# Projection, attention and feed-forward net in one block: the first maxima ahead of k's last spread, the first gates behind the last sums, late weights awaited where they are read

## The reference: what is computed

```python
q, k, v = x @ Wq.T + bq, x @ Wk.T + bk, x @ Wv.T + bv      # 16 heads of 16
q, k = rope(q), rope(k)
a = softmax(q @ k.T / sqrt(256)) @ v                        # 4096 x 4096 scores a head
x = layernorm(x + a @ Wo.T)
h = silu((x @ w1.T) * w1_s) * ((x @ w2.T) * w2_s)           # 256 -> 1024
h = gelu((h @ h1.T) * h1_s)                                 # 1024 -> 1024
h = gelu((h @ h2.T) * h2_s)                                 # 1024 -> 1024
x = layernorm(x + (h @ w3.T) * w3_s)                        # 1024 -> 256
```

## Time and profile before

| | us |
|---|---|
| median of 3 runs (3430.74 to 3432.02) | 3431.28 |
| the profiled execution | 3430.39 |
| its span | 3428.8 |
| PE busy | 3345.8 |
| DVE busy | 2985.9 |
| ACT busy | 2490.1 |

### The profile page before, as it was taken

How to read it: one execution, slowest core, us unless ns; L and a number is a source line. 1 busy time by engine, 2 the same in 40 slices (tenths; PEclk the granted TensorE clock), 3 DMA queues, 4 the chain that set the end, 5 groups by cost and what they waited for, 6 DMA issues and landing times. The chain is left out here.

```text
span 3428.8 us, 66866 instructions
## 1 busy us (share of the span) xinstructions
PE 3345.8 (98%) x28054; PEld 1529.5 (45%) x28054; DVE 2985.9 (87%) x3116; ACT 2490.1 (73%) x4521; POOL 128.0 (4%) x288
## 2 busy tenths in 40 slices
PE   9689999999999999999999999999999999999998
PEld 5233333333333333333333333333333288888887
DVE  8899999999999999999999999999999145555554
ACT  5248888888888888888888888888888822222222
POOL 0000000000000000000000000000000000000000
PEclk9679999999999999999999999999999999999999
DMA  4200000000000010001000000000002020000000
GB/s 157 76 4 13 13 12 13 25 13 18 25 12 14 11 62 12 13 13 61 13 13 30 13 13 13 13 12 13 12 8 94 13 91 26 26 26 26 26 13 13
DMA packets 47618, 92.04 MB, mean 27 GB/s; under 512 B 9922, under 2 KB 21828, under 8 KB 47140
## 3 DMA queue, kind: packets, MB, share of 16 engines
q1 hardware_dynamic: 40628, 72.07, 6.7%
q0 software_dynamic: 6688, 15.68, 1.6%
HBM read 69.62 MB, written 28.84 MB: 29 GB/s over the span
## 5 line engine op out<-in xcount | busy, mean ns | idle before, releaser
L886 DVE TENSOR_REDUCE group_max<-wide 128x2 f32<-128x1024 f32 x2048 | 2473.2, 1223 | 16.0 <-PE wide L656 9.4
L857 ACT ACTIVATE probs<-scores 128x512 f32<-128x512 f32 x4046 | 2199.6, 597 | 293.1 <-PE scores L780 41.3
L678 PE MATMUL sums<-probs,v_all 128*17 128x256 f32 (+1 forms) x16120 | 1278.4, 389 | 7.2 <-ACT mixed L837 6.3
L780 PE MATMUL scores<-q_sb,k_all 51*128 51x512 f32 x3968 | 988.6, 495 | 6.7 <-ACT probs L857 5.7
L656 PE MATMUL wide<-k_all,q_sb 48*128 48x512 f32 x4096 | 850.2, 411 | 33.5 <-DVE group_max L886 26.7
L780 PEld LDWEIGHTS scores<-q_sb,k_all 51*128 51x128 f32 x3968 | 370.5, 183 | 842.3 <-ACT probs L857 828.9
L678 PEld LDWEIGHTS sums<-probs,v_all 128*17 128x17 f32 x16120 | 267.1, 95 | 747.3 <-issue 367.5
L656 PEld LDWEIGHTS wide<-k_all,q_sb 48*128 48x128 f32 x4096 | 397.5, 190 | 72.4 <-DVE group_max L886 63.9
L1221 ACT ACTIVATE whole_hid<-acc,scale 128x512 f32<-128x512 f32 x128 | 84.6, 688 | 286.3 <-PE acc L1111 286.1
L1111 PE MATMUL acc<-hid_a,first_h1T 128*128 128x512 f32 x1024 | 233.5, 389 | 2.9 <-issue 2.9
L1111 PE MATMUL acc<-hid_b,h2T 128*128 128x512 f32 x1024 | 234.9, 390 | 0.0
(11 more groups left out here) (121 smaller groups left out, 1075.9 us busy)
## 6 DMA issues: line engine op xcount, KB each, us to landing
q_sb<-q_parts SPq DMA_DIRECT2D x192, 64.0 KB, 2.5
heads<-mixed SPq DMA_DIRECT2D x128, 34.0 KB
xt<-in_xT SPq DMA_DIRECT2D x8, 512.0 KB, 4.4
q_parts<-k_all SPq DMA_DIRECT2D x8, 512.0 KB, 3.3
q_parts<-parts SPq DMA_DIRECT2D x8, 512.0 KB, 3.3
w_words<-in_h1T POOLq DMA_DIRECT2D x32, 128.0 KB, 2.3
w_words<-in_h2T POOLq DMA_DIRECT2D x32, 128.0 KB, 2.3
heads_sb<-heads SPq DMA_DIRECT2D x16, 256.0 KB
```

The lines of the kernel that those rows point to most:

```text
L678: last = pe.matmul(sums[32 * j:32 * j + HD + 1, cols], v_all[:, kt, g, j], probs[(kt * HG + j) % RING][:, cols], start=(kt == 0 and cols.s ...
L780: pe.matmul(scores[(s + e) % BANKS][:], k_all[rows, g * GP + j, n // HG * P:(n // HG + 1) * P], q_sb[g][rows, j], start=True, stop=True).t ...
L857: act.activation(probs[n % RING][:], bank, ACT.Exp, scale=INV_SCALE)\
L886: dve.reduce_max(group_max[:, n], wide[n % 2][:], AX_X).then_inc(wide_free, 1)
```

## The change

One block is opened in `build` and handed to the three functions, so the two barriers between them are gone, and what they ordered is now ordered by semaphores, which live to the end. In `project`, q of group 0 is placed after item 14 is stored, groups 1 to 3 after item 15 is stored; the last spread is handed to `attend` as `before["spread_last"]`, and PE issues it after the first two groups of maxima. SBUF and PSUM tiles are placed in another order, so that what attention writes first doesn't lie on what projection reads last: `table` moves to the end, `probs` behind `bits`, and three of the four PSUM tiles of the spread move to the banks of `scores`. At the net's start PE waits for w1T, w2T and h1T, ACT and DVE for the small tables (before, SP waited for them ahead of the barrier); h2T and w3T are awaited where a layer reads them.

```diff
@@ project
-        block = ctx.enter_context(nc.Block())
...
                     for b in range(2):
                         sp.wait_ge(q_stored[b], 16)
-                    for g in range(NG - 1):
-                        place_q(sp, q_dram, q_sb[g], 0, g, q_in[g])
-            for b in range(2):
-                sp.wait_ge(q_stored[b], 16 * NCH * FT // 2)
+                    place_q(sp, q_dram, q_sb[0], 0, 0, q_in[0])
+
+            sp.wait_ge(v_ready, 2 * NCH)
+            for g in range(1, NG):
+                place_q(sp, q_dram, q_sb[g], 0, g, q_in[g])
...
-            for n in range(TOTAL + 2):
-                if n < TOTAL:
-                    item_of(n)
-                    values(n // FT, n % FT)
+            for n in range(TOTAL):
+                item_of(n)
+                values(n // FT, n % FT)
                 if n >= 2:
-                    spread_k(n - 2)
+                    spread_k(pe, n - 2)
+            spread_k(pe, TOTAL - 2)
@@ attend
-        probs = [sb(f"probs{r}", [P, CH]) for r in range(RING)]
...
         bits = sb("bits", [P, PIECE], I32)
+        probs = [sb(f"probs{r}", [P, CH]) for r in range(RING)]
...
-            load_q(0, NG - 1)
+            for b in range(2):
+                sp.wait_ge(before["q_stored"][b], 16 * (before["total"] // 2))
             place_shift(0, 0)
...
-            sp.wait_ge(w0_in, 16 * len(EARLY_W))
-            sp.wait_ge(small0_in, 16 * SMALL)
...
             pe.wait_ge(ident_set, 2)
+
+            pe.wait_ge(before["spread_free"], before["first_keys"])
+            pe.wait_ge(before["biased"], 2 * before["total"])
+            pe.wait_ge(before["v_free"], 2 * NCH)
             for n in range(MAXG):
                 max_group(0, 0, n)
+                if n == 1:
+                    before["spread_last"](pe)
+            pe.wait_ge(before["spread_free"], before["keys"])
...
+            dve.wait_ge(before["low_done"], before["total"])
             dve.memset(bits[:], 0).then_inc(scanned, 1)
             maxima(0)
 
+            dve.wait_ge(before["spread_free"], before["keys"])
             dve.memset(sums[:], 0.0).then_inc(sums_free, 1)
@@ feed_forward
                 def hidden_layer(c, layer):
+                    if layer == 1:
+
+                        pe.wait_ge(w_in["h2T"], 16)
...
+                    pe.wait_ge(w_in["w3T"], 16)
                     pe.wait_ge(hid_ready, c * HIDS + HIDS - 1)
...
+                pe.wait_ge(fc.w_in, 16 * len(EARLY_W))
                 gate_layer(0)
-                for name in w_in:
-                    pe.wait_ge(w_in[name], 16)
...
+            act.wait_ge(fc.small_in, 16 * SMALL_IN)
             gates(0)
...
+            dve.wait_ge(fc.small_in, 16 * SMALL_IN)
             dve.sem_inc(divided, FT)
```

More of the change, by code:

```diff
@@ L45 @@
     W_TOTAL += _rows * _cols
+SMALL_IN = 1 + 4 + 1
 EARLY_W = ("w1T", "w2T", "h1T")
@@ L84, in sem @@
         def sem(name):
-            return ctx.enter_context(nc.semaphore(name))
+            return kept.enter_context(nc.semaphore(name))
         TOTAL = NCH * FT
@@ L96, in project @@
         two_rows = sb("two_rows", [P, P], F32R)
-        table = [sb(f"table{p}", [P, 2, CH]) for p in range(2)]
         item = [sb(f"item{b}", [P, 2, CH]) for b in range(2)]
@@ L103, in project @@
         ones_rows = sb("ones_rows", [P, 1])
+        table = [sb(f"table{p}", [P, 2, CH]) for p in range(2)]
+        spread = [psum(f"ps_spread{j}", [P, CH]) for j in range(JP - 1)]
         ps = [psum(f"ps_{t}", [P, CH]) for t in "qk"]
         psv = [psum(f"ps_v{a}", [P, 2, D]) for a in range(2)]
-        spread = [psum(f"ps_spread{j}", [P, CH]) for j in range(JP)]
+        spread.append(psum(f"ps_spread{JP - 1}", [P, CH]))
         w_in = [sem(f"w_{t}_in") for t in "qk"]
@@ L195, in _, with spread_k @@
             pool.memset(v_all[:, :, :, :, HD:HD + 1], 1.0).then_inc(ones_set, 1)
+        def spread_k(pe, i):
+            if i == 0:
+                pe.wait_ge(choose_set, 5)
+            pe.wait_ge(low_done, i + 1)
+            if i > 0:
+                pe.wait_ge(spread_free, JP * i)
+            for a in range(2):
+                for j in range(JP):
+                    rows = slice(j * ROWS, (j + 1) * ROWS)
+                    last = pe.matmul(spread[j][:], choose[rows, a], parts[i % 2][rows, a, 1],
+                                     start=(a == 0), stop=(a == 1))
+                    if a == 1:
+                        last.then_inc(spread_ready, 1)
         @block.tensor
@@ L357, in _ @@
             low(TOTAL - 1)
+        return {"total": TOTAL, "spread_last": lambda pe: spread_k(pe, TOTAL - 1), "first_keys": JP * (TOTAL - 1), "keys": JP * TOTAL,
+                "spread_free": spread_free, "biased": biased, "v_free": v_free, "low_done": low_done, "q_stored": q_stored}
 class FirstChunk:
@@ L598, in _ @@
             pool.sem_inc(part_step, ROUNDS)
+            pool.wait_ge(before["low_done"], before["total"])
             pool.memset(ones[:], 1.0).then_inc(ident_set, 1)
@@ L945, in _, with feed_forward @@
             dve.wait_ge(x1t0_step, 2 * FT)
-def feed_forward(nc, io, heads_dram, shares_dram, w_dram, ident, first_chunk, last_stored, out):
+def feed_forward(nc, io, heads_dram, shares_dram, w_dram, block, ident, first_chunk, last_stored, out):
     with ExitStack() as ctx:
```

27 lines of the change are left out of this document (12 added, 15 removed).

## The result

| kernel | median, us | lowest to highest | executions |
|---|---|---|---|
| before | 3431.65 | 3430.74 to 3433.57 | 4 |
| after | 3415.61 | 3412.61 to 3416.39 | 4 |

The ratio is 0.9947 [0.9934, 0.9959]: faster, by 16.0 us in the medians, which is 0.5%. The profiled execution of after took 3415.28 us with a span of 3413.7, which is 15.1 less than the span of before. The forecast was 3415.5.

The account below looks back on a forecast made before the run. PE and DVE pace attention and PE the net, so only the two seams count: 7.45 first seam, 2.9 hole, 2.15 clock in the gates, 2.88 late weights, sum 15.4 us; forecast 3415.5, range 3412.5 to 3418.5.

Parts of the forecast that it names:

- Start of the first maxima: First seam: without the barrier PE starts the first maxima at 119.2 instead of 126.86, a gain of 7.66 us.
- input (b): First seam: DVE's increments that free `wide`, behind its last split, needed by PE's first maxima; expected at 118.8 to 119.3.
- The spread: First seam: of the last spread's 1.23 us, 1.0 lies beside DVE's reductions and 0.2 is on the path.
- The clock's rise: First unit: clock rises as late after the unit's start as before, costing nothing; 1 us either way is worth 0.46.
- The hole ahead of the gates: Second seam: PE's hole of 3.88 us shrinks to 1.0 for the flag load and branch, gaining 2.9 (2.5 to 3.9).
- Rival (1): Second seam: the clock falls all the same and the 2.15 us is not won, 3417.6; chance 16%.
- ACT's table load hidden: Second seam: ACT's table load and first product finish before PE needs the bank, with 0.7 us to spare.
- The late weights: Net, behind the first gates: awaiting h2T and w3T where they are read removes the whole hole of 2.88 us.
- `shares`, nothing: Net, chunk 1 on DVE: the wait for `shares` costs nothing, or 2 us if DVE's splits don't hold.
- Rival (2): Net: `shares` or the late weights bind after all, without the 2.88 and with 2 us lost on DVE, 3420.4; chance 5%.
- Rival (3), probs at other addresses: Attention's sums: reads of moved `probs` cost 1% more, 24 us, 3439, chance 3%; or 1% less, 3391, chance 2%.
- Rival (4): First seam: maxima still wait for all of q or the store; that seam gives about 2, 3421.5; chance 3%.

Follow-up runs that it names:

- the four corners: Kernels with or without the second barrier, late weights awaited behind the gates or where read; last sums to hidden layer: 23.57, 20.08 or 21.13, 24.31, 14.72 us.
- the first experiment: The changed kernel, but PE awaits h2T and w3T behind the first gates again, as before; median 3427.41 us, ratio 0.9982 against before.

## Why the prediction was right, and where only by sizes

**Start of the first maxima, 7.66.** Measured 7.82: 119.04, where I said 119.2. This trace puts the release down to q of group 0, one of the three inputs named. Of the two that come last, q lands at 118.81 and DVE's last split ends at 118.92. In the eight other traces without the first barrier PE starts 0.16 to 0.26 behind the end of that split, and they name POOL's `ones`, which waits for the same split and which PE doesn't need here. So it is as likely DVE's increments, input (b), as q, and no run parts the two. The run with SP's old order gives the same start, the run with the barrier back gives 130.46. The mechanism holds.

**The spread, 0.2 on the path.** The turn of the maxima came 7.77 earlier, so 0.05 was on the path. Putting the spread first costs 1.24. Mis-sized by 0.15: PE was back for the third group at 121.35, which is 2.31 after its start and not 2.45, and had it ready 0.84 later, at 122.19. DVE's second reduction started at 121.01; at its step of 1.13 the third would have started at 122.14. I had taken the lengths of PE's rows, 1.22 and 1.23, where its next work starts 1.15 and 1.16 behind theirs.

**The clock's rise, zero to within 0.46.** This bound is the step that failed. It came 4.6 us later after the unit's start than in the trace of before (11.3 instead of 6.7), and 2.35 of the 7.77 were gone by the first shift; at 0.46 a microsecond the 4.6 account for 2.1 of them. I took one execution's rise as the kernel's. The table shows that it isn't.

**The hole ahead of the gates, 1.0 left.** Measured 0.09. The load of `flag` and the branch show no time of their own: PE's first gate weights are loaded at 2731.96, 0.06 behind the last sums, so both ran beside these or inside that 0.06. So the gain is 3.79, not 2.9, inside the bounds of 2.5 to 3.9. This error and the one of the clock have opposite signs, and that is why 3415.5 lies so close to 3415.6; a good part of the closeness is luck, the more so as the four executions of after lie 3.8 apart.

**The clock in the gates, 2.15.** Measured 16.80 - 14.63 = 2.17, at 1.00 in every stretch from 2728 to 2748. Rival (1) is false here. The run with the barrier back shows the fall that goes with a hole of 3.98.

**ACT's table load hidden, with 0.7 to spare.** PE started at 2731.99; the load began at 2733.24, DVE's first product ended at 2736.09, and PE needed that bank at 2731.99 + 5 x 0.914 = 2736.56. The spare was 0.5, and 64 matmuls in 14.63 show no hole. The Trainium skill, "ScalarE: Activation LUTs", What ACT_TABLE_LOAD costs, puts a drain of about 1.38 us beside the load: the trace disagrees, with 1.28 for the load and the activation 1.29 after the load's start.

**The late weights, 2.88.** Measured 2.88: no hole. w3T landed at 2734.58 + 21.6 = 2756.2, 19.6 before PE ended the first hidden layer at 2775.79. It isn't a term of its own: with the barrier gone, awaiting them behind the gates costs 9.6, 11.3 with the clock, and not 2.88, as the four corners show.

**`shares`, nothing.** DVE's wait was long, but it ended at 2762.50, 7.6 earlier than before: 6.1 by the earlier sums, and 1.5 more against them (30.6 behind their end instead of 32.1):

```profile
2762.50 0.69 DVE L1291 TENSOR_TENSOR heads_sb<-heads_sb,shares 128x512 f32<-128x512 f32 x1 [11.81 <-DMA shares<-shares_dram]
```

Rival (2) is false. **Rival (3), probs at other addresses:** the groups of sums have the same mean as before:

```profile
L680 PE MATMUL sums<-probs,v_all 128*17 128x256 f32 (+1 forms) x16120 | 1279.3, 389 | 7.2 <-ACT mixed L846 6.3 <-ACT probs L866 0.9
```

389 ns and 1279.3 us over 16120, against 389 and 1278.4, 0.07% more where 0.6% would have decided. (The sums come in groups of 8 matmuls, 16120 by about 1990, not of 4 as I wrote; the price of 12 ns a group holds.) **Rival (4)** asked whether the maxima would wait for the store: it was issued at 118.95 and took 3.1 to land, and they began 0.09 after its issue. It is false too.

## What to carry to other kernels

At the first seam the barrier was as late as SP's queue ahead of it: the landing of a store issued at 122.45 in before, the last of 18 issues at 129.36 with the projection in its own block. To price one, read what the slowest queue ahead of it still has to do, and compare it with the inputs that the first instruction behind it really has. Before adding up gains of parts, look for a transfer that lands at a fixed time: everything saved ahead of it is waited for until its wait moves too. At the second seam taking out the barrier alone lost 0.7, 2.3 with the clock, and it gave 5.4 to 6.4 once the late weights were awaited where they are read. And a term from the clock's rise needs more than one execution.

## What the runs showed of the hardware

Two things I had not expected. The first group of sums at the full clock came between 3.6 and 18.7 us after the first sums in executions whose instructions there were the same or nearly so; in the longest, PE was busy 16.00 of the 16 us from 211 to 227 at a granted clock of 0.50. PE at 24.85 us busy of 25 ahead of the unit was granted the half level all the same. And a load of a flag with a compare and branch on PE left 0.09 us idle between two groups of matmuls, where with the barrier in the same place it was 3.9 to 4.0 and the clock fell to the half level. Over the hole of 9.44 us in the first experiment the clock fell too: 0.50 over 2759 to 2761, and 128 matmuls of the hidden layer took 30.86 instead of 29.2. Over the hole of 2.88 in before it stayed at 1.00.
